# Another order of TensorE's, VectorE's and the other engines' work within a chunk of a fused SSD and feed-forward layer

## The reference

```
x = x + mamba(layernorm(x));  x = x + ffn(layernorm(x))
mamba: gate, xBC, dt = split(x @ in_proj.T)       # 8192 | 8192 + 2*8*128 | 128
  xBC = silu(causal conv of 4 taps (xBC) + conv_b) # -> hs (128 heads x 64), B, C (8 groups x 128)
  chunked scan, per head: y_intra = ((C B^T) * decay * dt) x
                          y_inter = (C * exp(cum)) state;  state = cdec * state + (dt*dlast*B)^T x
  y = y_intra + y_inter + D * x
  g = y * silu(gate); g = g * rsqrt(mean over the group (g*g) + eps) * norm_w;  out = g @ out_w.T
ffn: w2(silu(w1 x) * (w3 x)), each with a LoRA of rank 16, hidden size 1376
```

## Time and profile before

| | us |
|---|---|
| median of 3 runs | 1844.99 (1844.36 to 1846.1) |
| profiled execution, its own time | 1847.52 |
| its span, first to last instruction | 1845.7 |
| TensorE busy | 1786.4 (97%) |
| VectorE busy | 1220.1 (66%) |
| ScalarE busy | 1159.4 (63%) |
| GpSimd busy | 1093.8 (59%) |

### The profile page before, as it was taken

How to read it: one execution, slowest core, us unless ns; L and a number is a source line. 1 busy time by engine, 2 the same in 40 slices (tenths; PEclk the granted TensorE clock), 3 DMA queues, 4 the chain that set the end, 5 groups by cost and what they waited for, 6 DMA issues and landing times.

```text
span 1845.7 us, 27457 instructions
## 1 busy us (share of the span) xinstructions
PE 1786.4 (97%) x9826; PEld 1437.3 (78%) x9826; DVE 1220.1 (66%) x2081; ACT 1159.4 (63%) x2218; POOL 1093.8 (59%) x1011
## 2 busy tenths in 40 slices
PE   7899999999999999999999999999999999899999
PEld 5678887888777877888787877887778777687777
DVE  5687677766786768666876777667766687563213
ACT  4676667666766677666766676667666776552411
POOL 4365666666656667575656666666566674673510
PEclk9999999999999999999999999999999999999999
DMA  3643334434533244333533354344333443243201
GB/s 115 177 137 93 116 100 152 120 113 121 151 106 116 87 134 139 107 120 109 159 91 115 106 152 120 108 125 150 96 122 87 134 144 108 82 113 113 74 15 46
DMA packets 121878, 211.01 MB, mean 114 GB/s; under 512 B 24240, under 2 KB 28976, under 8 KB 121744
## 3 DMA queue, kind: packets, MB, share of 16 engines
q1 hardware_dynamic: 121744, 209.26, 37.9%
HBM read 204.48 MB, written 4.72 MB: 113 GB/s over the span
## 4 chain that ended last, share of the span: by engine, by line
PE 82%; DVE 10%; POOL 4%; issue 2%; ACT 1%; DMA 1%; SPq 0%; DVEq 0%
PE bank L1488 16%; PE bank L1490 15%; PE bank L1489 14%; PE bank L1555 6%; PE bank L1568 5%; PE bank L1593 5%; PE bank L1595 4%; PE bank L1594 4%; PE bank L1581 4%; PE bank L1533 3%; DVE ow_l L1233 3%; DVE x_ch L1227 2%; DVE bcT L1227 2%; POOL xw L674 2%; DVE xdt L1246 1%
## 5 line engine op out<-in xcount | busy, mean ns | idle before, releaser
L1488 PE MATMUL bank<-x_h,w_h 128*128 128x512 f32 x1336 | 540.2, 404 | 18.3 <-DVE x_ch L1227 9.4
L656 POOL TENSOR_TENSOR w_l<-w_raw,w_h 128x512 fp32r<-128x512 f32 x288 | 374.9, 1306 | 290.7 <-ACT w_h L819 290.2
L1490 PE MATMUL bank<-x_h,w_l 128*128 128x512 f32 x1336 | 524.6, 393 | 0.0
L1489 PE MATMUL bank<-x_l,w_h 128*128 128x512 f32 x1336 | 524.1, 392 | 0.0
L1227 DVE SCALAR_TENSOR_TENSOR x_ch<-bank,par,x_ch 128x511 f32<-128x511 f32 (+2 forms) x384 | 287.3, 748 | 103.0 <-ACT x_ch L837 93.9
L1488 PEld LDWEIGHTS bank<-x_h,w_h 128*128 128x128 f32 x1336 | 252.5, 189 | 93.3 <-issue 20.2
L872 ACT ACTIVATE decay<-decay,cols 128x128 f32<-128x128 f32 x1024 | 317.4, 390 | 0.8
L1490 PEld LDWEIGHTS bank<-x_h,w_l 128*128 128x128 f32 x1336 | 252.3, 189 | 56.0
L1489 PEld LDWEIGHTS bank<-x_l,w_h 128*128 128x128 f32 x1336 | 252.8, 189 | 48.8
L662 POOL TENSOR_SCALAR_AFFINE_SELECT decay<-decay 128x512 f32<-128x512 f32 x256 | 203.3, 807 | 102.5 <-DMA decay<-cum_scratch 102.2
L1593 PE MATMUL bank<-ow_h,gT_h 128*128 128x512 f32 x512 | 222.5, 435 | 0.1
(11 more groups left out here) (140 smaller groups left out, 2667.4 us busy)
## 6 DMA issues: line engine op xcount, KB each, us to landing
w_raw<-in_wp SPq DMA_DIRECT2D x288, 256.0 KB, 3.4
decay<-cum_scratch SPq DMA_DIRECT2D x256, 256.0 KB, 4.1
ec<-ecum_scratch SPq DMA_DIRECT2D x96, 256.0 KB, 5.1
ow_raw<-in_ow SPq DMA_DIRECT2D x64, 256.0 KB, 5.1
w_raw<-in_w SPq DMA_DIRECT2D x48, 256.0 KB, 2.8
acc<-in_x SPq DMA_DIRECT2D x8, 256.0 KB, 5.6
out<-acc SPq DMA_DIRECT2D x8, 256.0 KB, 2.0
cols<-cols_scratch SPq DMA_DIRECT2D x16, 96.0 KB, 2.7
```

What stands on the lines that cost most here:

```text
L656: pool.tensor_tensor(w_l[:, s, :], w_raw[:, s, :], w_h[:, s, :].bitcast(F32), ALU.subtract).then_inc(wl_ready, 1)
L1488: pe.matmul(dst, wh, xh, start=(k == 0), stop=False)
L1489: pe.matmul(dst, wh, xl, start=False, stop=False)
L1490: last = pe.matmul(dst, wl, xh, start=False, stop=(k == len(terms) - 1 and not more))
```

## The change

It computes the same and has the same instructions of every kind; their order within a slot, and a few places, differ.

- `SLOT_TILES`: two convolution tiles in the first slot, four in the second and third, none in the fourth; gates 3, 1, 1, 3.
- TensorE, c < 3: `inside`, `new_state`, `square_total` of the chunk before, then a projection, then `turn_x`, `match`, `across` of the next chunk, then the rest. For c = 3 `turn_x` and `match` come after the first of three projections. In the first slot of all, the first projection goes ahead of `inside`.
- `mean_square`, `inverse_root` and `accumulate` of a chunk are done in the next slot. The sum of squares has a column of `cbb` instead of one of `xt[0]` (`xt[1]` in the slot `MIDDLE`, the fourth of the last group).
- VectorE: `fade` first (that of k = 1 in slot 0), `add_state` directly after `add_skip` and ahead of `gated`; `scale_across` ahead of the scores.
- GpSimd: two masks together, masks after `gT_low` at k = 0, `inverse_root` of the chunk before after the first `w_low`.
- SP: `ec` directly after `decay`; `ow` tiles 4 and 5 ahead of `decay` and 6 and 7 behind the first weight load.
- Last group: moments and inverses of chunks 0 and 1 in the third slot, their apply, transposes and split in the fourth, chunk 2's spread over it; in the first slot of the last unit `new_state`, `turn_x` and the norm transpose come ahead of the low-rank product.

```diff
-SLOT_TILES = [[("g", 0), ("c", 0), ("c", 1), ("c", 2), ("g", 1)],
-              [("g", 2), ("c", 3), ("c", 4), ("c", 5), ("g", 3)],
-              [("g", 4), ("c", 6), ("c", 7), ("c", 8), ("g", 5)],
-              [("c", 9), ("g", 6), ("g", 7)]]
+SLOT_TILES = [[("g", 0), ("g", 1), ("c", 0), ("c", 1), ("g", 2)],
+              [("c", 2), ("c", 3), ("c", 4), ("c", 5), ("g", 3)],
+              [("c", 6), ("c", 7), ("c", 8), ("c", 9), ("g", 4)],
+              [("g", 5), ("g", 6), ("g", 7)]]
...
 # VectorE, body
+                    if k != 1:
+                        fade(g, k)
                     add_skip(g, k)
+                    add_state(g, k)
+                    if not first:
+                        mean_square(*before)
...
                     gated(g, k)
                     taps_of(tiles[:1])
+                    scale_x(gn, kn)
                     if k == 0:
-                        for j in range(OW_EARLY):
+                        for j in range(OW_EARLY // 2):
                             ow_low(g, j)
-                    fade(g, k)
+                    if not first:
+                        accumulate(*before)
+                    if k == 0:
+                        for j in range(OW_EARLY // 2, OW_EARLY + 2):
+                            ow_low(g, j)
+                        fade(gn, kn)
...
                     taps_of(tiles[1:2])
-                    if more:
+                    if k > 0:
+                        scale_across(gn, kn)
                         scores(gn, kn, 0)
                         scores(gn, kn, 1)
                     taps_of(tiles[2:3])
-                    add_state(g, k)
                     if k == 0:
-                        for j in range(OW_EARLY, CT):
+                        scale_across(gn, kn)
+                        for j in range(OW_EARLY + 2, CT):
                             ow_low(g, j)
+                        scores(gn, kn, 0)
+                        scores(gn, kn, 1)
+                    scores(gn, kn, 2)
...
 # TensorE, new_state: waits for the transposed x of this chunk, no longer for that of the next
-                pe.wait_ge(xdt_ready, K + 2)
+                pe.wait_ge(xdt_ready, K + 1)
...
 # TensorE, turn_x: waits until the state has left the banks
-                if some(K - 1):
+                if some(K):
                     pe.wait_ge(xdt_ready, K)
-                    pe.wait_ge(mean_ready, K - 1)
+                    pe.wait_ge(state_ready, n_state(g, k))
...
 # TensorE, last_chunk
                 inside(LAST, k)
+                new_state(LAST, k)
+                if k > SC:
+                    square_total(LAST, k - 1)
                 if k == SC:
                     turn_x(LAST, k + 1)
+                    norm_transpose(1, k - 1)
                     match(LAST, k + 1)
-                    norm_transpose(1, k - 1)
+                    across(LAST, k + 1)
...
 # TensorE, body
+                    first = not some(g * CHUNKS + k)
+                    if first:
+                        projects(tiles[:1])
                     inside(g, k)
-                    projects(tiles[:1])
-                    if c == SC - 1:
-                        projects(tiles[1:2])
-                        if last:
+                    new_state(g, k)
+                    if not first:
+                        square_total(*((g, k - 1) if k else (g - 1, CHUNKS - 1)))
+                        if last and c == SC - 1:
                             norm_transpose(1, 0)
                             norm_transpose(1, 1)
-                        projects(tiles[2:])
-                        if last:
-                            norm_transpose(1, 2)
-                        turn()
+                        projects(tiles[:1])
+                    turn_x(gn, kn)
+                    match(gn, kn)
+                    if c == SC - 1:
+                        projects(tiles[1:])
                         out_half(g, k, 0)
+                        if last:
+                            norm_transpose(1, 2)
+                            square_total(g, k)
                         out_half(g, k, 1)
-                        square_total(g, k, more)
                         continue
-                    turn()
+                    across(gn, kn)
                     projects(tiles[1:3])
-                    new_state(g, k)
                     out_half(g, k, 0)
                     projects(tiles[3:-1])
-                    across(gn, kn)
-                    square_total(g, k, more)
                     if k == 0:
                         projects(tiles[-1:])
                         out_half(g, k, 1)
-                        continue
-                    out_half(g, k, 1)
-                    projects(tiles[3:][-1:])
+                    else:
+                        out_half(g, k, 1)
+                        projects(tiles[-1:])
```

More of the change, by code:

```diff
@@ L603, in body @@
                         load_next_w(g, last, b, i)
[L604 to L607, removed]
+                    if k == 0:
+                        load_ow(g, range(OW_EARLY + 2, CT))
                     for i in tiles[1:-1]:
@@ L1078, in body @@
                         continue
+                    if c == SC - 1:
+                        if last:
+                            norm_high(1, 0)
+                            norm_high(1, 1)
+                        tile(tiles[:1])
+                        gT_high(g, k)
+                        square(g, k)
+                        copy_b(gn, kn)
+                        for q in range(QUARTERS):
+                            exps(gn, kn, q)
+                        if last:
+                            norm_high(1, 2)
+                        tile(tiles[1:])
+                        if k == CHUNKS - 1:
+                            for j in range(OW_EARLY):
+                                ow_high(g + 1, j)
+                        continue
                     tile(tiles[:1])
@@ L1369, in last_chunk @@
                 pairs = LAST_PAIRS[k]
-                norm_moments(1, k - 1)
-                if k > SC:
-                    gate_up(pairs[0] - 1)
+                if k == SC:
+                    add_skip(LAST, k)
+                    add_state(LAST, k)
+                    norm_apply(1, k - 1)
+                    gated(LAST, k)
+                    norm_low(1, k - 1)
+                    scale_x(LAST, k + 1)
+                    scale_across(LAST, k + 1)
+                    low_low(0)
+                    for q in range(QUARTERS):
+                        scores(LAST, k + 1, q)
+                    gate_up(pairs[0])
+                    return
+                gate_up(pairs[0] - 1)
+                fade(LAST, k)
                 add_skip(LAST, k)
-                if k == SC:
-                    norm_apply(1, k - 1)
+                add_state(LAST, k)
+                mean_square(LAST, k - 1)
                 gated(LAST, k)
@@ L1428, in body @@
                         continue
-                    late = range(SC - 1) if last and c == SC - 1 else []
-                    for cc in late:
-                        norm_moments(1, cc)
-                    add_skip(g, k)
+                    late = last and c == SC - 1
+                    before = (g, k - 1) if k else (g - 1, CHUNKS - 1)
+                    first = not some(g * CHUNKS + k)
+                    if late:
+                        norm_apply(1, 0)
+                        norm_apply(1, 1)
@@ new lines, in body @@
+                    if last and c == SC - 2:
+                        norm_moments(1, 0)
+                        norm_moments(1, 1)
+                    if late:
+                        norm_moments(1, 2)
+                        scores(gn, kn, 0)
+                        norm_apply(1, 2)
+                        for q in range(1, QUARTERS):
+                            scores(gn, kn, q)
+                        mean_square(g, k)
+                        norm_low(1, 2)
+                        accumulate(g, k)
+                        norm_moments(1, c)
+                        continue
@@ L1451, in body @@
                     taps_of(tiles[2:3])
[L1452 removed]
                     if k == 0:
[L1454 removed]
+                        scale_across(gn, kn)
+                        for j in range(OW_EARLY + 2, CT):
                             ow_low(g, j)
[L1456 to L1460 removed]
+                        scores(gn, kn, 0)
+                        scores(gn, kn, 1)
+                    scores(gn, kn, 2)
+                    if k == 0:
                         scores(gn, kn, 3)
[L1462 to L1464 removed]
+                        taps_of(tiles[3:-1])
+                    else:
+                        taps_of(tiles[3:-1])
+                        scores(gn, kn, 3)
             body(0, False)
```

232 lines of the change are left out of this document (108 added, 124 removed).

## The result

Measured: 1814.53 us (1812.41 to 1815.71, four runs) against 1845.55 (1844.36 to 1847.02, four runs) for the kernel before; the ratio is 0.983 (95% interval 0.9813 to 0.9847). That is 31.0 us less, where 40 were forecast. The forecast of 1805 was 9.5 too low. The measured time lies within the stated range (1794 to 1818), but 1.5 above the band of 1797 to 1813. The profiled execution took 1815.39, its span is 1813.6, and the mean granted clock is 0.996.

The account below looks back on a forecast made before the run. TensorE, busy 97%, was taken as the bound, VectorE in slots k = 0. Gains 4.1 + 18.0 + 7.0 + 4.3 + 6.8 = 40.2 turn the 1845.7 span into 1805.5, own time 1807.3, median 1805; range 1794 to 1818.

Parts of the forecast that it names:

- rival A: Shared access of VectorE and GpSimd takes the k=0 gain: slots at 28.4 or 29.9, time 1812 to 1822; chance 0.20.
- Usual slots: Slots k = 1, 2, 4, 5, 6: fewer changes of matmul kind save 0.11 in each of 37, 4.1 us.
- I take 0.03: Usual slots: assumed cost of the new joins I to N and M to A, between 0 and 0.13 us.
- Rival B: The joins cost as much as the exits saved, above all I to N: 1811 us; chance 0.07.
- Slots 3 and 7: Fifteen slots k = 3 and 7 lose their waits and take 17.25 us: gain 1.2 each, 18.0 us.
- dead heat: Slots k = 3 and 7: gT_low ends at 11.6, just when O0 comes; 0.15 us added for it.
- Slot k = 0: Seven slots bound by VectorE lose one set of taps: 27.4 for 28.44, gain 7 us (-10 to +16).
- the 1.56 case: Slot k = 0: ow_low at 1.56 us each, with GpSimd at work through all six; the slot takes 29.9.
- Around the last unit's start: Last group's slot 3 gains 2.2 and the last unit's first slot 4.6, together 6.8 us (3 to 10).
- + 3.0: Last unit's first slot: T waits 1.5 for add_state, and norm_apply meeting lbT costs about 1.5 more.
- Rival C: All waits vanish, slot k = 0 at 26.1 included: 1792 us; chance 0.09.
- Rival D: Slower: the chain N, add_state, T sets the pace; T waits 1.0 in 59 slots, 1864 us; chance 0.03.

Follow-up runs that it names:

- The repair: Under 2: kernel after with gT_low ahead of the last two masks in slots k = 3 and 7, 1808.46 us; under 5: the third repair.
- the third repair: Kernel after with GpSimd's lbT product moved behind gT_low in the last unit's first slot: 1809.85 us.
- the repairs: Kernel after with four moves together: fade of k = 1 back in slot 1, gT_low before masks, lbT product later, norm transpose later: 1798.54 us.

## Why the prediction was right, point by point

The direction and the place of the time were right: no usual slot waits, T waits for `add_state` only in the first slot of all and the last unit's first, and slots k = 3 and 7 bring most. The size owes something to the width of the range: the time lies in the 1812 to 1822 of rival A, whose mechanism didn't occur (k = 0 takes 27.1, not 28.4 or more). One sign of being wrong came up as well: T starts 6.70 into the usual slot, but A 7.90, later than the 7.8 named, and by the joins of point 1, not by a wait.

Between the forecast sum (40.2) and the measured one (32.1) lie 8.1 us, with the 1.2 of scatter ahead of the first `turn_x` counted as gain; the slots alone fall 9.3 short. The terms carry the following shares. The rest of the 9.5 is that I put the median 2.5 below the profiled execution, and here it is 0.9 below.

1. *Usual slots, 4.1 forecast, 3.1 measured.* The step that failed is "I take 0.03" for the joins I to N and M to A. The saved changes brought 0.15 (O0 0.04, O1 0.11) and a shorter A 0.07, 0.22 in all; the joins cost 0.10 (N 1.82 for 1.72) and 0.08 (M 0.33 for 0.25), and P0 gave 0.02: 0.06, where the slots show 0.07. Rival B was right in mechanism for I to N and too dear in sum. The 0.10 shows more plainly in k = 3, where S behind I takes 0.24 and behind N or A 0.14. The Trainium skill, "TensorEngine Tiling (Array Packing)", section "Key Properties", says that a change of tiling mode drains the array; the 0.10 on leaving the 64-column tiles for full plain ones agrees, though no run here changed the tiling alone. Part of the measured 3.1 (0.45) is one slot of before that took 26.67. The 4.9 us said to be left beside `gT_high` and `gT_low` are 5.15 by the same figures (15.1 - 6.5 - 1.05 - 2.40), which changes nothing here.
2. *Slots 3 and 7, 18.0 forecast, 12.2 measured, the largest miss.* There are 14 such slots and not 15, since the last group's slot 3 and the last slot stand under other terms: 1.2 of the 5.8 is this slip. S behind I costs 0.10 that the sum lacked, and P0 0.03. The "dead heat" was one: `gT_low` ends at 861.77, O0 starts 0.14 late and takes 0.14 more itself, so 0.27 and not 0.15, and twice `gT_low` came later still. The repair returned 0.27 a slot, and 4.8 in all. TensorE, S and the start of P0, then the last matmul of P2 and the first of O0:

```profile
851.89 0.38 PE L1662 MATMUL bank<-ones,y 128*128 128x1 f32 x2
852.13 0.48 PE L1540 MATMUL bank<-x_h,w_h 128*128 128x512 f32 x1
...
861.46 0.39 PE L1542 MATMUL bank<-x_h,w_l 128*128 128x512 f32 x1
861.82 0.50 PE L1651 MATMUL bank<-ow_h,gT_h 128*128 128x512 f32 x1
```

3. *Slot k = 0, 7.0 forecast, 7.5 measured.* Right in size, in part by luck: the slot came out 0.3 below the forecast's 27.4, but the 28.44 it started from is the longest of the seven, whose mean is 28.16. Rival A is out. Of the two PE waits forecast, only O1's came (0.60); the taps were in time because the six `ow_low` took 6.96 together, 1.16 each and not 1.31. That what GpSimd does beside `ow_low` is the cause is shown by the shortened `gT_low` (26.15). The Trainium skill, "SBUF — State Buffer", section "Who interferes with whom", has the exclusive pair; the 2.22 over `gT_low` agrees: `ow_low` starts at 878.66 and ends 0.54 after `gT_low` does (880.34). Beside the masks, which have one SBUF input, `ow_low` is slowed from 0.74 to 1.12 only, less than that section would have it, so the whole of GpSimd's work doesn't count alike, and the 1.56 case didn't come.
4. *First slot, 4.3 forecast, 4.2 measured.* The clock is at full as said (before, it was at its lower level from 98 to 103 us), though T waits 1.5 for `add_state`.
5. *Around the last unit's start, 6.8 forecast, 5.0 measured.* Slot 3 is exact at 18.75, with two errors that cancel: O0 doesn't wait here, which the forecast's 17.25 had at 0.15, and S and P0 take the 0.13 of point 2. In the next slot (2.8 of the 4.6, and by the traces named under the third repair perhaps 1.7) the step that failed is "+ 3.0": T's 1.5 came, but `norm_apply` stood 3.27 and not 2.9 and cost 2.0 instead of 1.5, and "the lower clock gone" was half wrong: 3.4 us at the lower level cost A 1.36 (3.07 for 1.71). The repair shows both belong to the `lbT` product.
6. *"Slots 5 to 7 of the last unit and the feed-forward end: same work, 0".* The last slot lost 1.1: `norm_transpose` came 0.8 earlier than `norm_apply` was ready. Moving it gave 0.9 back. I had costed the slots by their work and not checked each moved call for its producer.

Rival C (all waits vanish) came near only with the repairs: 1798.5 measured, where it said 1792, with T's two waits of 1.5 and the one of 1.1 left in the scan's slots. Rival D did not occur; but the run with the old tiles is its mechanism in another place, at fifteen times 3.9 us.

The tiles alone give 14 of the 31 us, 12 of it in slots 3 and 7; the other 17 are the order's, and only on top of the tiles. In those 17 the usual slots have 5.6, the first slot of all 3.9 (from the first `turn_x`) and the last unit's first slot 3.9. Why the usual slots of the tiles-only kernel take 0.07 more isn't shown. The largest part is A, 1.86 where it took 1.78, and it starts 0.14 after `add_state` ends (944.97, 944.83), where it had 0.46 before (957.44, 956.98). Where A did wait 1.1 for `add_state`, in k = 0 of the kernel before, it took 1.86 as well, so a wait too short for the view is likely.

## What to carry to other kernels

Before grouping calls of one kind on a pipelined engine, read both sides of a change: the call behind it pays an entry, but the call ahead of it looks shorter by about as much, so the net price was 0.014 us here and not 0.13. Look for the gain in the waits, and for every call moved forward write down its producer's end in each kind of slot, the rare ones too: each of the four waits repaired here was for one late producer, and repairing them gave half as much again as the change. Parts that share a precondition can't be judged alone: the order without the tiles cost 85 us.

## What the runs showed of the hardware

- A plain-float call takes longer from start to start when another plain call follows than when a split product does: `match` 0.33 and 0.25, `across` 1.78 and 1.71. Half or more of the entry that the split product shows (0.10 to 0.14) is given back there, and one plain stretch more cost 0.014 net.
- Leaving `inside` (64-column tiles) for a full plain product costs 0.10 (S 0.24 for 0.14, N 1.82 for 1.72, all of it in its first matmul); for a split product it costs 0.13 to 0.14, as the entry behind other plain calls does (P1 behind M 0.13).
- A VectorE `tensor_scalar` of 0.65 took 3.27 beside a GpSimd product on 32 partitions only: few partitions didn't make the neighbour harmless.
- After waits of 1.5 and 2.0 us, 1.0 apart, the granted clock went to its lower level for 3.4 us; after single waits of 0.6 in slots k = 0, and after the 1.5 alone in the first slot, it did not.
